# Flamingo block on one Trainium2 core: the weights of an expert block in one transfer instead of two, and two block tables built earlier

## The chip, the cores and the metric

The kernel runs on one core of one Trainium2 chip. The metric is the device time of one execution in microseconds (us). Each time named "span" is that of a profiled execution, from its first to its last instruction.

## The reference

The reference takes x of 8 x 256 x 128 floats (2048 tokens of 128 features) through four residual steps: a cross attention of 16 heads, a mixture-of-experts integrator of two iterations (8 experts, 2 per token), a second cross attention without weights, and a mixture of 8 gated experts. The change lies in the last step, and in how its work is laid out:

```python
def _L1_ffn_ref(x, Wr, br, W1, b1, W2, b2, W3, b3):
    E, D, DFF = (8, 128, 512)
    b, s, d = x.shape
    xt = x.reshape(b * s, d)
    logits = xt @ Wr + br
    pr, idx = jax.lax.top_k(logits, 2)
    w = jax.nn.softmax(pr, axis=-1)
    onehot = jax.nn.one_hot(idx, W1.shape[0], dtype=x.dtype)
    cw = jnp.einsum('tk,tke->te', w, onehot)
    y = jnp.zeros_like(xt)
    for e in range(W1.shape[0]):
        h = jax.nn.silu(xt @ W1[e] + b1[e]) * (xt @ W2[e] + b2[e])
        y = y + (h @ W3[e] + b3[e]) * cw[:, e:e + 1]
    return y.reshape(b, s, d)
```

## The kernel before

The 2048 tokens stand in four chunks of 512 (NC = 4, the last is called L). Each token has two experts, so there are 4096 rows. They are sorted by expert into `sorted_x` in DRAM, each expert's rows in a region of its own, and worked on in blocks of 128 rows of one expert, 39 in all (BLOCKS). The blocks don't wait for all tokens to be routed: a table gives the expert and the start row of each block, and it is made in three parts. The early table (9 blocks, EARLY) holds blocks that the first two chunks fill, the middle table (8) those that are full after the third chunk, the late table (22) the rest. Block numbers 9 and 17 are the first of the middle and of the late table.

What each engine does in the stretch of the blocks:

- TensorE, loop from L2265: for block j `up(j)` (eight products of 128 x 128 by 128, shown as 16 MATMULs in the trace, L2247), then `rows_T` (the transpose of a later block's rows, L2237), then `down(j - 1)` (L2258). The order is fixed in the code, so a wait of one of these holds all behind it. `up(j)` waits for the weights `w_in`, `rows_T(j)` for the rows `xb_in`. At a table border the transposes come later: `rows_T(9)` stands between `up(8)` and `down(7)`.
- ScalarE: the four silu of a block (L1087) and the copy of the transposed rows (L1078).
- VectorE, loop from L1649: the four `gated` products (L1655), then `keep_result(j - 1)` (L1647), and between them small pieces of routing: `choose(L)` at j = 2, `weights_of(L)` and `slots_of(L)` at j = 3 (the first waits for GpSimd's `w_top`, L804), `blocks_of(1)` at j = 4, the middle table at j = 5, `blocks_of(2)` at j = 7, the late table at j = 8.
- GpSimd, loop from L820: the indirect store of a block's result (L823), and between them the indirect stores of the third chunk's rows (L798, three before the loop, then two behind blocks 0 and 1 and one behind block 2), the power for the last chunk's weights `second_weights(L)` (L804) behind those of j = 1, and the last chunk's rows behind blocks 3 to 6.
- SyncE issues the loads, in the order of its program: for each block `load_weights` and `load_rows`. Each starts with a value load from the table (L598). The weights of a block are 772 KB, in two transfers: W1, W2 and the two biases (516 KB, L605) and W3 (256 KB, L608). There are four buffers (W_BUFS). From block 4 on, the first transfer waits for `gated` of four blocks ago, the second for the down product of four blocks ago. Rows (65 KB, L614) are loaded three blocks ahead (AHEAD). `load_blocks` (L633) starts a table: it waits for the table (the wait in L634), then issues weights, waits for the sent rows of that chunk, and goes on. The trace puts a block's value loads, and with them the wait for a table, at L598.

Of the kernel before, what the change touches and what calls it, by code (L numbers as in the profile page):

```python
# [50 lines left out]
B1_AT, B2_AT, W3_AT = 2 * FF, 2 * FF + MT, 2 * FF + 2 * MT  # L51
W_BUFS, X_BUFS = 4, 10
EARLY_CHUNKS = 2
EARLY = (2 * EARLY_CHUNKS * CH - E * (P - 1) + P - 1) // P
MIDDLE = (2 * (EARLY_CHUNKS + 1) * CH - E * (P - 1) + P - 1) // P - EARLY
# [24 lines left out]
def flamingo(nc, a, out):  # L80
    ctx = ExitStack()
    with ctx:
# [3 lines left out]
        def sem(name):  # L86
            return ctx.enter_context(nc.semaphore(name))
# [299 lines left out]
        shareT_ready = sem("shareT_ready")  # L387
        bias3_psum = sem("bias3_psum")
        w_in = [sem(f"w_in{i}") for i in range(W_BUFS)]
        w3_in = [sem(f"w3_in{i}") for i in range(W_BUFS)]  # L390
        xb_in = [sem(f"xb_in{i}") for i in range(X_BUFS)]
        xbT_psum = sem("xbT_psum")
        xbT_ready = sem("xbT_ready")
# [103 lines left out]
        def _(sp):  # L497
# [102 lines left out]
            def load_weights(j):  # L600
                expert = entry(j, 0, E - 1)
                w = a["wall"][bass.ds(expert, 1)].rearrange("o p n -> (o p) n")
                if j >= W_BUFS:
                    sp.wait_ge(gated_ready, MT * (j - W_BUFS + 1))
                sp.dma_start(wb[:, j % W_BUFS, 0:W3_AT], w[:, 0:W3_AT]).then_inc(w_in[j % W_BUFS], 16)  # L605
                if j >= W_BUFS:
                    sp.wait_ge(down_psum, j - W_BUFS + 1)
                sp.dma_start(wb[:, j % W_BUFS, W3_AT:], w[:, W3_AT:]).then_inc(w3_in[j % W_BUFS], 16)  # L608

            def load_rows(j):  # L610
                start = entry(j, 1, SLOTS - P)
# [53 lines left out]
        def _(pool):  # L665
# [135 lines left out]
            def second_weights(c):  # L801
                pool.wait_ge(gap2_ready, c + 1)
                tc = slice(c * TC, (c + 1) * TC)
                nc.gpsimd.tensor_tensor(w_top[:, tc, 1], euler[:, 0:TC], gap2[:, tc], ALU.pow).then_inc(w2nd_ready, 1)  # L804
# [15 lines left out]
            for j in range(BLOCKS):  # L820
                pool.wait_ge(yb_ready, j + 1)
                home = xb[:, j % X_BUFS, D:D + 1].bitcast(U32)
                nc.gpsimd.indirect_dma_start(sorted_y, bass.IndirectOffsetOnAxis(ap=home, axis=0), yb[:, j % X_BUFS, :],  # L823
                                             None).then_inc(yb_out[j % X_BUFS], 16)
                if j < 3:
                    send_rows(2, range(2 * j + 3, min(2 * j + 5, GR)))
                if j == 1:
                    second_weights(L)
                if 3 <= j < 7:
                    send_rows(L, range(2 * j - 6, 2 * j - 4))  # L830

# [270 lines left out]
        def _(dve):  # L1102
# [525 lines left out]
            choose(2)  # L1628
            weights_of(2)
            slots_of(2)  # L1630

            def expert_shares():

# [15 lines left out]
            for j in range(BLOCKS):  # L1649
# [14 lines left out]
                if j == 3:  # L1664
                    weights_of(L)
                    slots_of(L)
                if j == 4:
                    blocks_of(1)
                if j == 5:
                    table_of_blocks(1, middle_table, MIDDLE, middle_ready)  # L1670
                if j == 7:
                    blocks_of(2)
                if j == 8:
                    table_of_blocks(2, late_table, LATE, late_ready)
                if j == 10:
                    expert_shares()
# [15 lines left out]
        def _(pe):  # L1692
# [557 lines left out]

            def down(j):
                w = wb[:, j % W_BUFS, W3_AT:W3_AT + MT * D]
                pe.wait_ge(w3_in[j % W_BUFS], 16 * (j // W_BUFS + 1))
                pe.wait_ge(gated_ready, MT * (j + 1))
                if j:
                    pe.wait_ge(yb_ready, j)
                for m in range(MT):
                    last = nc.tensor.matmul(bank[4][:, 0:D], gated[:, j % 2, m, :], w[:, m * D:(m + 1) * D],  # L2258
                                            start=(m == 0), stop=(m == MT - 1))
                last.then_inc(down_psum, 1)  # L2260
# [133 lines left out]
```

## Time and profile before

| | us |
|---|---|
| median of 3 runs | 654.27 |
| lowest, highest | 643.7, 655.16 |
| the profiled execution, device time | 628.24 |
| its span | 626.4 |
| mean granted TensorE clock in it, share of full speed | 0.961 |

The views of the profile that are used: the page's digits, each the busy share of one fortieth of the span (15.7 us) in tenths; the waits, which name who stood idle and what ended the wait; the timelines of single engines, each line a start in us, a duration, the engine, the source line, the operation, the number of instructions merged, and in brackets the idle time before it with what ended it; and for a source line that issues transfers the time from issue to landing. A landing is not known for every transfer, so its median is that of those known.

### The profile page before, as it was taken

How to read it: one execution, taken by the hardware profiler on the slowest of the kernel's cores; microseconds unless marked ns; L12 is line 12 of the kernel's file. 1: busy time of each engine (PE TensorE's matmuls, PEld its weight loads, DVE VectorE, ACT ScalarE, POOL GpSimd, SP SyncE). 2: the span in 40 equal slices, each digit the busy share in tenths (PEclk: the TensorE clock that was granted, in tenths of full speed). 3: DMA queues.
4: the chain of work that ended last, by engine and by line, in shares of the span. 5: the costliest groups of instructions: out<-in, count | busy, mean ns of one | idle time of the engine just before them, and what ended most of it. 6: DMA issues, size and time to landing. Idle time of an engine off the chain costs nothing. (4 is left out here: it accounts for less than half of the span.)

```text
span 626.4 us, 10027 instructions
## 1 busy us (share of the span) xinstructions
PE 556.1 (89%) x3331; PEld 327.0 (52%) x3343; DVE 413.5 (66%) x1054; ACT 321.3 (51%) x652; POOL 206.9 (33%) x217
## 2 busy tenths in 40 slices
PE   3856899999998799999999999999977989999991
PEld 1422344444453244444444445545556978988981
DVE  4858978989348599677323665656887675444545
ACT  2624656666657875565445437274533534444430
POOL 4806801010023363001783220001465575323330
PEclk9886979999999999999999999999999899999996
DMA  8466693000019700000003002000003989989956
GB/s 277 119 172 103 160 197 53 2 4 3 2 65 321 258 0 1 1 0 0 0 16 119 0 1 20 0 1 0 23 25 112 288 263 296 311 278 321 321 208 209
DMA packets 48011, 71.21 MB, mean 114 GB/s; under 512 B 11110, under 2 KB 35112, under 8 KB 47672
## 3 DMA queue, kind: packets, MB, share of 16 engines
q1 hardware_dynamic: 44968, 65.61, 36.0%
q0 software_dynamic: 2272, 4.69, 2.1%
q8 instruction: 27, 0.44, 0.3%
q10 hardware_dynamic: 720, 0.27, 0.2%
q14 instruction: 24, 0.20, 0.1%
HBM read 59.18 MB, written 21.29 MB: 128 GB/s over the span
## 5 line engine op out<-in xcount | busy, mean ns | idle before, releaser
L1963 PE MATMUL psum<-hidden,ew 128*128 128x512 f32 x320 | 143.8, 592 | 0.6
L886 ACT ACTIVATE probs<-psum 128x512 f32<-128x512 f32 x128 | 74.6, 598 | 47.5 <-PE psum L1765 47.1
L1963 PEld LDWEIGHTS psum<-hidden,ew 128*128 128x128 f32 x320 | 60.7, 190 | 69.3 <-issue 68.1
L1172 DVE TENSOR_REDUCE negmax<-psum 128x4 f32<-128x1024 f32 x64 | 76.7, 1209 | 19.4 <-PE psum L1742 18.7
L2247 PE MATMUL psum<-xbT,wb 128*128 128x128 f32 x624 | 78.5, 280 | 3.0 <-DMA wb<-in_wall_dram 2.9
L2247 PEld LDWEIGHTS psum<-xbT,wb 128*128 128x128 f32 x624 | 74.3, 195 | 4.3 <-DMA wb<-in_wall_dram 4.1
L1087 ACT ACTIVATE silu_g<-psum,wb 128x128 f32<-128x128 f32 x156 | 44.6, 368 | 61.6 <-PE psum L2247 61.6
L1655 DVE SCALAR_TENSOR_TENSOR gated<-psum,wb,silu_g 128x128 f32<-128x128 f32 x156 | 43.9, 344 | 48.6 <-ACT silu_g L1087 46.5
L823 POOL DMA_INDIRECT sorted_y<-yb,xb x39 | 37.9, 972 | 66.8 <-DVE yb L1647 65.6
L1765 PE MATMUL psum<-stacks 50*128 50x256 bf16 x256 | 50.4, 287 | 4.1 <-issue 1.9
L768 POOL TENSOR_TENSOR hidden<-unmasked,chosen 128x512 f32<-128x512 f32 x16 | 24.5, 1534 | 60.1 <-ACT unmasked L936 59.0
L1778 PE MATMUL psum<-probs,v_aug 128*32 128x256 f32 x512 | 44.1, 409 | 0.0
L2258 PE MATMUL psum<-wb,gated 128*128 128x128 f32 x312 | 41.5, 276 | 1.5 <-DVE yb L1647 1.5
L2258 PEld LDWEIGHTS psum<-wb,gated 128*128 128x128 f32 x312 | 37.9, 192 | 2.0 <-issue 2.0
L798 POOL DMA_INDIRECT sorted_x<-xp,slot x32 | 31.8, 995 | 17.9 <-DVE slot L1529 9.6
L1349 DVE SCALAR_TENSOR_TENSOR soft<-psum,soft 128x512 f32<-128x512 f32 x24 | 16.2, 687 | 31.6 <-ACT soft L950 31.6
L1765 PEld LDWEIGHTS psum<-stacks 50*128 50x128 bf16 x256 | 18.8, 98 | 33.4 <-issue 16.8
L1742 PE MATMUL psum<-stacks 48*128 48x256 bf16 x256 | 30.7, 297 | 5.8 <-DMA stacks<-stacked 5.6
L1908 PE MATMUL psum<-xT,ew 128*128 128x512 f32 x64 | 32.8, 600 | 1.3 <-ACT routeT L908 1.3
L672 POOL TENSOR_SCALAR rstd<-meanvar 128x4 f32<-128x4 f32 x16 | 3.8, 240 | 89.5 <-DVE meanvar L1110 89.4
L962 ACT ACTIVATE sig_g<-psum 128x512 f32<-128x512 f32 x24 | 14.3, 596 | 35.1 <-PE psum L1963 35.1
L762 POOL TENSOR_TENSOR hidden<-hidden,chosen 128x512 f32<-128x512 f32 x16 | 22.2, 1416 | 20.1 <-DVE hidden L1336 20.1
(256 smaller groups left out, 955.5 us busy)
## 6 DMA issues: line engine op xcount, KB each, us to landing
wb<-in_wall_dram SPq DMA_DIRECT2D x39, 516.0 KB, 5.0
wb<-in_wall_dram SPq DMA_DIRECT2D x39, 256.0 KB, 4.4
sorted_x<-in_slots_dram SPq DMA_DIRECT2D x1, 9815.0 KB, 32.7
stacks<-stacked SPq DMA_DIRECT2D x12, 384.0 KB, 8.5
xb<-sorted_x SPq DMA_DIRECT2D x39, 65.0 KB, 3.7
stacked<-parts SPq DMA_DIRECT2D x6, 384.0 KB, 3.7
back<-sorted_y SPq DMA_DIRECT2D x4, 512.0 KB, 5.2
stacked<-parts SPq DMA_DIRECT2D x6, 256.0 KB, 3.6
```

The source lines that it names most:

```text
L798: nc.gpsimd.indirect_dma_start(sorted_x, bass.IndirectOffsetOnAxis(ap=slot[:, 2 * t + k:2 * t + k + 1], axis=0), xp[:, t, k, :], None).the ...
L823: nc.gpsimd.indirect_dma_start(sorted_y, bass.IndirectOffsetOnAxis(ap=home, axis=0), yb[:, j % X_BUFS, :], None).then_inc(yb_out[j % X_BUF ...
L886: nc.scalar.activation(probs[:, g % 2, h % 4, :, :], s2[n % 2].rearrange("p (k q) -> p k q", k=2), ACT.Exp, scale=float(HD) ** -0.5).then_ ...
L1087: nc.scalar.activation(silu_g[:, j % 2, m, :], bank[j % 2][:, m * P:(m + 1) * P], ACT.Silu, bias=wb[:, j % W_BUFS, B1_AT + m:B1_AT + m + 1 ...
L1172: nc.vector.tensor_reduce(negmax[:, p].rearrange("p h q -> p (h q)"), psum[:, i:i + 2, :].rearrange("p h (q k) -> p (h q) k", q=2), AX.X, ...
L1655: nc.vector.scalar_tensor_tensor(gated[:, j % 2, m, :], bank[2 + j % 2][:, m * P:(m + 1) * P], wb[:, j % W_BUFS, B2_AT + m:B2_AT + m + 1], ...
L1765: last = nc.tensor.matmul(s2[n % 2][:, k * S:(k + 1) * S], ks[rows, h // 2, b * S + k * P:b * S + (k + 1) * P], qs[rows, h // 2, b * S:(b ...
L1778: last = nc.tensor.matmul(o[b % 2][32 * j:32 * j + 32, (g // 2) * S:(g // 2 + 1) * S], v_aug[:, b % BC, k, 4 * g + j, :], probs[:, g % 2, ...
L1908: last = nc.tensor.matmul(dst, w[:, 0, :], xT[:, chunk(c)], start=True, stop=not it)
L1963: last = nc.tensor.matmul(dst, ew2[:, j, cols], hidden[:, c, k - 1, j, :], start=False, stop=(j == 3))
L2247: last = nc.tensor.matmul(bank[2 * i + j % 2][:, m * P:(m + 1) * P], w[:, i * FF + m * P:i * FF + (m + 1) * P], xbT[:, j % 2, :], start=Tr ...
L2258: last = nc.tensor.matmul(bank[4][:, 0:D], gated[:, j % 2, m, :], w[:, m * D:(m + 1) * D], start=(m == 0), stop=(m == MT - 1))
```

## The change

The two transfers of a block's weights become one, which waits for `gated` and for the down product of four blocks ago (for the latter last). The semaphores `w3_in` go; the down product waits for `w_in`, as the up product does. `blocks_of(1)` moves from block 4 to ahead of the loop, the middle table from j = 5 to j = 1, `blocks_of(2)` from j = 7 to j = 5, and the late table from j = 8 to j = 6. On GpSimd, `second_weights(L)` goes ahead of the two row sends of j = 1.

```diff
@@ load_weights (SyncE)
                 if j >= W_BUFS:
                     sp.wait_ge(gated_ready, MT * (j - W_BUFS + 1))
-                sp.dma_start(wb[:, j % W_BUFS, 0:W3_AT], w[:, 0:W3_AT]).then_inc(w_in[j % W_BUFS], 16)
                 if j >= W_BUFS:
                     sp.wait_ge(down_psum, j - W_BUFS + 1)
-                sp.dma_start(wb[:, j % W_BUFS, W3_AT:], w[:, W3_AT:]).then_inc(w3_in[j % W_BUFS], 16)
+                sp.dma_start(wb[:, j % W_BUFS, :], w[:, :]).then_inc(w_in[j % W_BUFS], 16)
@@ GpSimd's loop over blocks
+                if j == 1:
+                    second_weights(L)
                 if j < 3:
                     send_rows(2, range(2 * j + 3, min(2 * j + 5, GR)))
-                if j == 1:
-                    second_weights(L)
                 if 3 <= j < 7:
                     send_rows(L, range(2 * j - 6, 2 * j - 4))
@@ VectorE, ahead of its loop
             choose(2)
             weights_of(2)
             slots_of(2)
+            blocks_of(1)
@@ VectorE's loop
                 if j == 3:
                     weights_of(L)
                     slots_of(L)
-                if j == 4:
-                    blocks_of(1)
+                if j == 1:
+                    table_of_blocks(1, middle_table, MIDDLE, middle_ready)
                 if j == 5:
-                    table_of_blocks(1, middle_table, MIDDLE, middle_ready)
-                if j == 7:
                     blocks_of(2)
-                if j == 8:
+                if j == 6:
                     table_of_blocks(2, late_table, LATE, late_ready)
@@ down (TensorE)
-                pe.wait_ge(w3_in[j % W_BUFS], 16 * (j // W_BUFS + 1))
+                pe.wait_ge(w_in[j % W_BUFS], 16 * (j // W_BUFS + 1))
```

## Rows read from the trace of the kernel before

**Rows 1.** The page: the DMA engines' busy tenths by slice of 15.7 us.

```profile
DMA  8466693000019700000003002000003989989956
```

**Rows 2.** Waits from 485 to 612: total us, times, longest us.

```profile
PE psum L2237 <- DMA xb<-sorted_x: 4.8, 5, 2.0
...
PE psum L2247 <- DMA wb<-in_wall_dram: 2.9, 5, 1.2
```

**Rows 3.** Timeline of TensorE, at blocks 2, 5, 8, 10, 19, 20, 26, 27 and 38.

```profile
491.42 0.33 PE L2237 MATMUL psum<-ident,xb 128*128 128x128 f32 x1 [0.53 <-DMA xb<-sorted_x]
...
505.61 1.13 PE L2258 MATMUL psum<-wb,gated 128*128 128x128 f32 x8 [0.34 <-DVE yb L1647]
...
516.70 0.33 PE L2237 MATMUL psum<-ident,xb 128*128 128x128 f32 x1 [1.98 <-DMA xb<-sorted_x]
...
521.08 0.33 PE L2237 MATMUL psum<-ident,xb 128*128 128x128 f32 x1 [1.26 <-DMA xb<-sorted_x]
...
549.26 1.95 PE L2247 MATMUL psum<-xbT,wb 128*128 128x128 f32 x16
...
553.45 2.05 PE L2247 MATMUL psum<-xbT,wb 128*128 128x128 f32 x16 [1.24 <-DMA wb<-in_wall_dram]
...
572.41 1.95 PE L2247 MATMUL psum<-xbT,wb 128*128 128x128 f32 x16
...
574.30 1.06 PE L2258 MATMUL psum<-wb,gated 128*128 128x128 f32 x8
575.20 1.95 PE L2247 MATMUL psum<-xbT,wb 128*128 128x128 f32 x16
...
606.74 1.95 PE L2247 MATMUL psum<-xbT,wb 128*128 128x128 f32 x16
```

**Rows 4.** SyncE's own waits from 485 to 612: total us, times, longest us.

```profile
SPq L608 <- PE psum L2258: 8.0, 7, 1.7
SPq L598 <- DVE middle_table L1580: 2.5, 1, 2.5
```

**Rows 5.** Timeline of SyncE: issues for blocks 8, 9, 22 and 23.

```profile
506.91 0.33 SPq L608 DMA_DIRECT2D wb<-in_wall_dram  x1
...
512.14 1.44 SPq L614 DMA_DIRECT2D xb<-sorted_x  x2
...
555.22 0.34 SPq L605 DMA_DIRECT2D wb<-in_wall_dram  x1
555.74 0.33 SPq L608 DMA_DIRECT2D wb<-in_wall_dram  x1
...
557.94 0.34 SPq L605 DMA_DIRECT2D wb<-in_wall_dram  x1
```

**Rows 6.** Timeline of VectorE around blocks 0, 2, 4, 5 and 6.

```profile
489.03 1.12 DVE L1655 SCALAR_TENSOR_TENSOR gated<-psum,wb,silu_g 128x128 f32<-128x128 f32 x4 [2.08 <-PE psum L2247]
...
494.90 1.13 DVE L1655 SCALAR_TENSOR_TENSOR gated<-psum,wb,silu_g 128x128 f32<-128x128 f32 x4 [1.44 <-ACT silu_g L1087]
...
502.70 0.17 DVE L1510 TENSOR_SCALAR gap<-w_top 128x4 f32<-128x4 f32 x1 [1.23 <-POOL w_top L804]
...
508.04 0.16 DVE L1584 TENSOR_TENSOR ends<-ends,taken 128x8 f32<-128x8 f32 x1
...
510.27 1.13 DVE L1655 SCALAR_TENSOR_TENSOR gated<-psum,wb,silu_g 128x128 f32<-128x128 f32 x4
```

**Rows 7.** Timeline of GpSimd behind block 1's store.

```profile
500.64 0.96 POOL L798 DMA_INDIRECT sorted_x<-xp,slot  x1 [0.30 <-issue]
```

**Rows 8.** The chain that ended last: start, us, what (the rows of block 11).

```profile
516.07 4.96 DMA xb<-sorted_x
```

**Rows 9.** Line L608 (last 256 KB), issues from 568 to 612.

```profile
DMA to landing us min/median/max: 5.0/5.3/5.8
```

**Rows 10.** Line L605 (first 516 KB), issues from 568 to 612.

```profile
DMA to landing us min/median/max: 3.8/5.3/6.3
```

**Rows 11.** Line L608, issues from 512 to 550.

```profile
DMA to landing us min/median/max: 4.4/4.4/4.4
```

More of the change, by code:

```diff
@@ L389, in flamingo @@
         w_in = [sem(f"w_in{i}") for i in range(W_BUFS)]
-        w3_in = [sem(f"w3_in{i}") for i in range(W_BUFS)]
         xb_in = [sem(f"xb_in{i}") for i in range(X_BUFS)]
```

## The prediction

> **What bounds the kernel now.** I read the page first: its digits by slice show the DMA engines at 8 or 9 tenths from the 32nd slice to the 38th and nowhere else for so long [rows 1]. These are the 39 expert blocks, and everything the change touches lies there or just ahead of it. The waits of that stretch come next: TensorE stands still there 4.8 us for rows and 2.9 us for weights [rows 2]. The timeline of TensorE then says where, and how long a block takes when nothing is missing: from up(26) to up(27) 575.20 - 572.41 = 2.79 us [rows 3]. From up(19) at 549.26 to up(38) at 606.74 it takes 57.48 / 19 = 3.03 a block [rows 3]. So some 0.24 a block is lost late, and more in the first blocks and at the table borders. A block needs 772 KB of weights and 65 KB of rows; that the DMA digits stand at 9 [rows 1] says the transfers have little room either. Last, SyncE's own waits and timeline: it waits only 8.0 us for down products and 2.5 us for the middle table [rows 4], and between 555.22 and 557.94 it goes from one block's first weight transfer to the next in 2.72 us without a wait [rows 5]. It is a chain of value loads and three issues, nearly as long as a block, and when it is late (the weights of block 20, 1.24 us of wait at 553.45 [rows 3]) it can't catch up.
>
> **The change, part by part.**
>
> *One issue fewer.* The second issue starts 0.52 us behind the first (555.74 - 555.22 [rows 5]), so SyncE's chain falls from 2.72 to 2.20 us a block and is never the bound. In the first blocks it issues without waiting: the rows of block 3 come behind three weight loads, each with one issue less, 3 x 0.52 = 1.6 us earlier, and those of block 4 2.1 us earlier. TensorE waits 0.53 us for the first of them [rows 3] and nearly the same for the second; both go: -1.0.
>
> *Table work and GpSimd's order.* blocks_of(1) lands in front of block 0, where VectorE stands idle 2.08 us [rows 6]; it is five small operations, of which the trace's like take 0.16 to 0.3 us, at most 1.5 in all, so hidden. The middle table at j = 1 takes 2.2 us (508.04 to 510.27 [rows 6]) and falls into 1.44 us of idle time before 494.90 [rows 6]; gated(2) comes 0.8 us later, but down(2), which needs it, stands behind the whole of up(3), which has not begun: hidden. What now stands at j = 5 and 6, blocks_of(2) and the late table, takes the place of the middle table there, so nothing more is lost. second_weights(L) goes in front of two sends of 0.96 us each with 0.3 between [rows 7], 2.5 us earlier; VectorE's 1.23 us wait for it at 502.70 [rows 6] goes, and with it TensorE's 0.34 us at 505.61 [rows 3]. Two of GpSimd's row sends come 1.2 us later, the last one of the middle group does not, as it stood behind w_top already. With VectorE's other small shifts I count -0.5, so -1.5 by block 8.
>
> *The middle table's wait.* SyncE reaches the wait for the table behind the weights of block 8, at 506.91 + 0.33 = 507.3 [rows 5], and stands 2.5 us [rows 4]. That wait goes, but the weights of block 9 then wait for down(5). Down(4) ended at 505.61 + 1.13 = 506.74 [rows 3]; one block on, less the 1.5 us gained, down(5) ends at 508.0. So the weights go out at 508.2 and, half of SyncE's 2.2 us chain later, the rows of block 9 at 509.3 in place of 512.14 [rows 5]. From issue to transpose these took 516.70 - 512.14 = 4.6 us [rows 3, 5], which gives 513.8. TensorE wanted them at 516.70 - 1.98 = 514.7, now at some 512.9: 0.9 of the 1.98 us stay, and the transpose is 2.9 us earlier. The rows of block 11 sit behind the weights of block 10, which now wait for down(6), near 511.1: issued at 512.3, and 5.0 us later [rows 8] at 517.3, against 521.08 before [rows 3]. So block 10 starts 3.8 us earlier than before, of which 1.5 is counted: -2.3. At the border to the late table I count nothing: its rows stand behind a load that waited for a down product before too.
>
> *The later start of the weights.* Today the first 516 KB of block j may start at gated(j-4), and only the last 256 KB wait for down(j-4). Now all wait. SyncE issues 0.17 us behind a down product's end (505.61 + 1.13 = 506.74, and 506.91 [rows 3, 5]); that end lies 0.16 behind the next up's start (574.30 + 1.06 = 575.36 against 575.20 [rows 3]); up(j) comes two blocks behind this up. With p the time of a block and L the time from issue to landing, 2p = L + 0.37 with 0.04 from landing to start; and a block that wants 2.79 us allows L = 5.2. The merged transfer isn't in the trace. Bounds: no shorter than the second part alone, 5.3 in the last third [rows 9]; no longer than from the first issue to the second's landing, 0.5 + 5.3 = 5.8, with 6.3 as the longest of the first parts [rows 10]. Both parts land nearly together and the engines are busy, so bytes set it: I take 5.7, p = 3.03. Between 512 and 550 the second part landed after 4.4 [rows 11], so L = 4.9 and p stays 2.79: no wait there, nor in the early blocks.
>
> From up(19) to up(38) there are 19 periods. Block 20 keeps 1.0 of its 1.24 us (three row issues stand ahead of it in SyncE's chain). Four periods at 2.79 and fifteen at 3.03: 1.0 + 11.2 + 45.5 = 57.7 against 57.5: +0.2. SyncE's lateness is exchanged for a wait on the landing.
>
> The Trainium skill (DMA: Bandwidth & Descriptors, Anatomy of one DMA — SWDGE (gpsimd) path) gives a transfer about 2.0 us fixed plus its bytes at 436 GB/s, measured for the other issue path. That would be 3.8 us for these 772 KB. By it the 5.2 us are never reached and the fifteen periods cost 2.79. The trace does not agree: smaller parts took 5.3 here.
>
> **Sum.** -1.5 - 2.3 + 0.2 = -3.6 us. The profiled execution took 628.24 us (span 626.4 and 1.8 around it); it becomes 624.6. The runs' median is 654.27, 26 us over the profiled one, for which the trace gives no reason. I carry the difference over: 654.27 - 3.6 = 650.7.
>
> **Rivals.**
>
> *All hidden.* The merged transfer, with one start in place of two, lands in 5.2 us or less. Then 19 periods take 1.0 + 53.0 = 54.0, -3.5, and the whole -1.5 - 2.3 - 3.5 = -7.3: 647.0. For it: the 4.4 us of the middle stretch [rows 11]. Against: DMA engines at 9 tenths [rows 1]. Chance 0.2. The skill's fixed cost, above, would lead here.
>
> *Late weights (slower).* Every block now hangs on a landing that closes a loop of two blocks, and blocks are closer together before block 20 than they were, so queues are fuller. If L is 6.3, the longest seen [rows 10], p is 3.34 and the 19 periods take 63.5, +6.0; less 3.8 gained ahead, +2.2: 656.5. If blocks 12 to 19 go that way too, 8 x 0.55 = 4.4 more: 660.9. It decides from L = 6.1, where 19 periods cost what was gained. For it: landings rose from 4.4 to 5.3 as the blocks closed up [rows 9, 11]. Against: slower blocks load the engines less, which brings L down again. Chance 0.2.
>
> *The table is not the wait.* If the middle rows' sends, two of which come later, land behind SyncE's arrival, a wait for rows takes the place of the one for the table. The last send stands behind w_top and both of them in either order, so it is not later by its place; SyncE asks for it at 508.6, and another 1 us would be needed to bite. Then the -2.3 shrinks to nothing: -1.3, 653.0. Chance 0.1.
>
> **How the numbers follow.** My forecast, 650.7, has 0.5; its own range, L from 5.3 to 6.0, moves fifteen periods from 3.03 to 2.84 or 3.19, 647.8 to 653.1. The cases together reach from 647.0 to 660.9. The unprofiled runs of one program lie between 643.7 and 655.16, so the low end needs a few us below the cases: 642 to 660. Faster or slower by over 2% (13 us, about what a measurement of this kernel can tell from no change) lies outside every case: of the 127 us of this stretch 39 x 2.79 = 109 us are TensorE's at full pace, and the rest, 18 us, is all that there is to gain. I leave 0.05 for each, for what the trace doesn't show. The sign is more open than that: 0.75 for some gain.
>
> **What would show it.** Right, in the changed kernel: no wait of SyncE for the middle table; rows of block 9 issued some 3 us earlier; no 1.23 us wait of VectorE for w_top; SyncE waiting for down products in nearly every block, far over 8.0 us; TensorE's waits for rows down from 4.8 to about 1.5 to 2.5, its waits for weights at or above 2.9, spread over many small ones after block 24; landings of 772 KB near 5.7 us late and near 4.9 between. up(10) some 3.8 us earlier. Wrong: landings under 5.2 late (then all is hidden), or over 6.1 (then slower), a wait for the middle rows, or a new wait of TensorE on VectorE near blocks 2, 5 or 6 from the moved tables.

## The result, and the profile after

| | before | after |
|---|---|---|
| median, us | 642.2 (22 runs, 630.46 to 658.44) | 642.39 (22 runs, 635.56 to 661.68) |
| ratio after / before | | 1.0086, 95% interval 1.005 to 1.0123 |
| profiled execution, us | 628.24, span 626.4 | 636.66, span 634.9 |
| mean granted TensorE clock in it | 0.961 | 0.960 |

The change made the kernel 0.9% slower, some 5.5 us. That is within 2%, as forecast, but on the other side of zero: the forecast was -3.6 us. The ratio is of the executions alone in which the core was not in its slower state; the medians are of all 22, and so nearly alike.

The page after, the DMA engines' busy tenths by slice, which answers to [rows 1]:

```profile
DMA  8466792000059300000030001000117768899865
```

The waits of the kernel after from 485 to 620 (total us, times, longest us), which answer to [rows 2]; the up product is L2244 here, the transpose L2234, the down product L2255:

```profile
ACT silu_g L1085 <- PE psum L2244: 43.5, 26, 5.5
ACT silu_g L1085 <- issue: 22.4, 11, 3.0
DVE gated L1654 <- remote: 9.7, 2, 5.4
...
PE psum L2244 <- DMA wb<-in_wall_dram: 3.5, 8, 0.7
PE psum L2255 <- DVE yb L1646: 3.3, 3, 1.9
...
PE psum L2234 <- DMA xb<-sorted_x: 1.7, 2, 1.5
```

SyncE's own waits in the same stretch, which answer to [rows 4]:

```profile
SPq L605 <- PE psum L2255: 34.1, 25, 3.8
```

Much is as forecast. SyncE no longer waits for the middle table and waits 34.1 us for down products in place of 8.0; TensorE's waits for rows fell from 4.8 to 1.7 us and those for weights rose from 2.9 to 3.5, in small pieces. But two rows were not forecast: ScalarE waited up to 5.5 us for an up product and VectorE 5.4 us for a signal whose sender the trace does not name. Signals of this kind, that come several us after all that they need has ended, are called late signals below. From up(0) to up(10) this execution took 42.0 us and the one before 36.7; from up(10) to up(38) 87.9 and 84.6. So the first ten blocks, where the gain should be, seem to have lost 5 us, and the late ones 3.

One trace cannot say which of the two is the change. The experiments had to answer two questions: whose are the late signals in the first blocks, and what does the one transfer cost, which starts behind the down product.

### The profile page after: what moved, and what is told of

It reads as the page before. It is cut to its first block, busy times and chain, and to the rows that moved or that the text cites. A ratio compares the mean times of both kernels' runs of the same rounds, so it can differ in the third digit from the quotient of the medians.

```text
span 634.9 us, 9956 instructions
## 1 busy us (share of the span) xinstructions
PE 562.6 (89%) x3343; PEld 329.4 (52%) x3343; DVE 414.0 (65%) x1054; ACT 321.4 (51%) x652; POOL 206.9 (33%) x217
## 3 DMA queue, kind: packets, MB, share of 16 engines
q1 hardware_dynamic: 39352, 65.61, 35.3%
## 4 chain that ended last, share of the span: by engine, by line
PE 63%; DVE 10%; DMA 10%; SPq 7%; issue 4%; ACT 3%; POOL 2%; another core or an unknown queue 0%; DVEq 0%; POOLq 0%
PE psum L1960 21%; DMA wb<-in_wall_dram 5%; PE psum L2244 5%; PE psum L1905 5%; PE psum L1762 4%; PE psum L1775 4%; PE psum L2255 3%; PE psum L1907 3%; SPq L513 2%; PE psum L1957 2%; PE psum L1783 2%; PE psum L1739 2%; DVE negmax L1170 2%; DMA xb<-sorted_x 2%; PE psum L1789 1%
## 5 line engine op out<-in xcount | busy, mean ns | idle before, releaser
L1960 PEld LDWEIGHTS psum<-hidden,ew 128*128 128x128 f32 x320 | 60.7, 190 | 69.4 <-issue 68.1
L2244 PE MATMUL psum<-xbT,wb 128*128 128x128 f32 x624 | 81.2, 285 | 5.3 <-DMA wb<-in_wall_dram 3.5
L2244 PEld LDWEIGHTS psum<-xbT,wb 128*128 128x128 f32 x624 | 76.1, 199 | 8.0 <-DMA wb<-in_wall_dram 6.1
L2255 PE MATMUL psum<-wb,gated 128*128 128x128 f32 x312 | 41.8, 277 | 3.3 <-DVE yb L1646 3.3
L2255 PEld LDWEIGHTS psum<-wb,gated 128*128 128x128 f32 x312 | 37.9, 192 | 4.1 <-issue 3.9
L1905 PE MATMUL psum<-xT,ew 128*128 128x512 f32 x64 | 34.3, 626 | 0.0
L670 POOL TENSOR_SCALAR rstd<-meanvar 128x4 f32<-128x4 f32 x16 | 3.9, 241 | 89.4 <-DVE meanvar L1108 89.0
L960 ACT ACTIVATE sig_g<-psum 128x512 f32<-128x512 f32 x24 | 14.3, 596 | 35.1 <-PE psum L1960 35.1
```

Source lines behind the costliest of these rows:

```text
L1905: last = nc.tensor.matmul(dst, w[:, 0, :], xT[:, chunk(c)], start=True, stop=not it)
L1960: last = nc.tensor.matmul(dst, ew2[:, j, cols], hidden[:, c, k - 1, j, :], start=False, stop=(j == 3))
L2244: last = nc.tensor.matmul(bank[2 * i + j % 2][:, m * P:(m + 1) * P], w[:, i * FF + m * P:i * FF + (m + 1) * P], xbT[:, j % 2, :], start=Tr ...
```

## How the runs are compared

The span of an execution follows the granted clock: the kernel before took 633.2 us at a mean clock of 0.962 and 660.0 at 0.909 on one chip. Where the runs of a ratio happen to have unlike clocks, the plain ratio misleads: it is 1.022 for the kernel before against itself (e16, two runs). So each result below also has a "difference at equal clock": the kernels were measured in five groups, each on one chip and in one go, and for each group the spans of all runs were fitted with a parabola in the granted clock, common to its kernels, and one offset for each kernel against the kernel before. The offset is given in us with two standard errors.

A second column is read from the traces, the start of an up product to the start of another. The clock hardly touches these stretches: their rows show mostly the full pace of 1.95 us for the 16 products.

| kernel (edits) | ratio (95%) | difference at equal clock, us | up(0) to up(10) | up(10) to up(38) |
|---|---|---|---|---|
| **First chip** | | | | |
| e1 changed kernel | 1.0118 (1.0056 to 1.018) | +4.6 ± 1.7 | 45.4 | 87.5 |
| e2 merged transfer alone | 1.0201 (1.0163 to 1.0239) | +3.8 ± 1.9 | 41.9 | 88.8 |
| e3 tables and GpSimd's order alone | 1.0015 (0.9975 to 1.0054) | 0.0 ± 1.4 | 46.5 | 82.2 |
| e4 two transfers, both start late | 1.0051 (1.0003 to 1.0099) | +1.6 ± 1.5 | 42.6 | 89.4 |
| **Second chip** | | | | |
| e5 kernel before | | +1.6 ± 2.4 | 36.4 | 83.8 |
| e6 changed, five weight buffers | 0.9895 (0.9854 to 0.9935) | -6.7 ± 2.2 | 33.0 | 79.6 |
| e7 changed, rows ahead of weights | 1.0086 (1.0032 to 1.0141) | +3.7 ± 1.9 | 36.0 | 85.8 |
| e8 both edits of e6 and e7 | 0.9899 (0.9837 to 0.9961) | -4.2 ± 2.3 | 37.2 | 78.4 |
| **Third chip** | | | | |
| e9 kernel before | 1.0008 (0.9918 to 1.0098) | 0.0 ± 2.8 | 43.0 | 85.2 |
| e10 changed kernel | 1.0024 (0.9967 to 1.0081) | +3.6 ± 1.9 | 45.8 | 85.1 |
| e11 merged, five buffers, old tables | 0.9885 (0.9825 to 0.9944) | -4.8 ± 2.3 | 40.6 | 81.5 |
| e12 tables and order alone | 1.0014 (0.9942 to 1.0087) | +0.4 ± 2.2 | 44.9 | 82.0 |
| **Fourth chip** | | | | |
| e13 GpSimd's order alone | 0.9985 (0.9929 to 1.004) | -2.6 ± 1.5 | 35.3 | 84.9 |
| e14 tables alone | | +0.6 ± 2.3 | 34.5 | 84.2 |
| e15 changed kernel | 1.0048 (1.0001 to 1.0096) | +2.6 ± 1.6 | 34.0 | 88.7 |
| e16 kernel before | 1.022 (1.0164 to 1.0275) | -1.4 ± 3.1 | 36.2 | 83.4 |
| **Fifth chip** | | | | |
| e17 merged, five buffers, new order, old tables | 0.9895 (0.9703 to 1.0088) | -5.5 ± 2.3 | 35.1 | 79.0 |
| e18 changed, five buffers | 0.9815 (0.968 to 0.9951) | -8.7 ± 2.7 | 32.4 | 79.9 |

The changed kernel was measured three times beside the kernel before, on three chips: +4.6, +3.6, +2.6. Weighted by their errors that is +3.6 ± 1.0 us. Fitted with the runs at a clock of 0.94 and more alone they are +5.4 ± 1.7, +4.2 ± 1.9 and +3.1 ± 1.9, so the sign does not rest on the runs at a low clock. Only e2 has no run at 0.94 or more: its offset is the least certain of the table.

## Experiment: whose late signals are these?

The kernel before and the changed one, both unchanged, on the third chip and again on the fourth.

> The kernel before, unchanged, profiled beside the next three. Open is where the late signals in blocks 1 to 9 come from (in the profiles of the changed kernel, of the merged transfer alone, of the tables alone and of the split transfer started late, up(0) to up(10) took 42 to 46.5 us; in two profiles of the kernel before and three with other edits 33 to 37). If they belong to the chip or to the single execution, the kernel before can show them too: up(0) to up(10) over 41 us, where all kernels of this group show it. If they belong to the merged transfer or the moved tables, this one takes 36 to 37 us and the changed kernel beside it 42 or more. Compared at the same granted clock its span is within 2 us of the other runs of the kernel before.

> The changed kernel, unchanged, beside the kernel before on one chip. Theory (the late start of the weights, with the borders): at the same granted clock it is 3 to 6 us longer than the kernel before; up(19) to up(38) takes 57.2 to 58.2 us, up(10) to up(38) 86 to 88. If the late signals are the chip's, up(0) to up(10) is within 2 us of that of the kernel before beside it; if they are the change's, it is 4 us or more longer. Rival (the first blocks are what costs the time and the late ones nothing): up(10) to up(38) as in the kernel before.

The kernel before took 43.0 us from up(0) to up(10) here: it has the late signals too. These are its ScalarE and VectorE around block 7, timelines of two engines (the silu of block 7 is the first line):

```profile
517.03 1.14 ACT L1087 ACTIVATE silu_g<-psum,wb 128x128 f32<-128x128 f32 x4 [2.26 <-PE psum L2247]
522.84 1.14 ACT L1087 ACTIVATE silu_g<-psum,wb 128x128 f32<-128x128 f32 x4 [4.67 <-remote]
```

```profile
517.03 0.34 DVE L1647 TENSOR_SCALAR yb<-psum,xb 128x128 f32<-128x128 f32 x1
522.65 1.13 DVE L1655 SCALAR_TENSOR_TENSOR gated<-psum,wb,silu_g 128x128 f32<-128x128 f32 x4 [5.28 <-remote]
```

Silu(7) ends at 518.17, and gated(7), which needs nothing later, starts at 522.65, 4.5 us on. In the first profile of the kernel before, gated(7) came without a wait. The same kernel, again profiled on the fourth chip, does not have this:

> The kernel before again, for its profile on this chip. Whether up(0) to up(10) takes 36 to 37 us or 43 here tells which kind of chip this is; the three others are read against it. If the two kinds go by chip, all four kernels of this call show the late signals or none does.

> The changed kernel again, beside the parts. 3 to 5 us longer than the kernel before at the same granted clock; up(19) to up(38) 56.8 to 58.2 us. On a chip without the late signals up(0) to up(10) is 36 us or less, on one with them 42 to 46.

Here up(0) to up(10) took 36.2 us before and 34.0 after. All eight profiles on the first and the third chip show 40.6 to 46.5 us, all ten on the other three chips 32.4 to 37.2, whatever the kernel. The kernel before also has different times at equal clock there: at 0.95 the fits give it 636.5 and 635.9 us on the first and the third chip, 627.2, 628.7 and 628.4 on the others. So the late signals come with all kernels of a group or with none, not with an edit, and where they come the span is some 8 us longer, 6 to 7 of them in the kernel before from up(0) to up(10) (43.0 against 36.2 to 36.7). Each chip was measured in one go only, so whether it is the chip or the time is not separated; "chip" stands for both here. The profile after that is shown above has them and the one before has not. Read against each other without this control, the two would have put 5 us on the wrong account. What makes the signals late on such a chip the runs do not show.

On a chip with late signals the moved tables and order also seem to stretch the first blocks: 42.0, 45.4, 45.8 (changed kernel), 46.5 and 44.9 (tables alone) against 43.0, 41.9, 42.6 and 40.6 in four kernels with the old tables. It is one execution each and the groups overlap, so this stays a hint.

## Experiment: the parts of the change

The merged transfer alone (the change's edits to load_weights and down, and nothing else):

```diff
-                sp.dma_start(wb[:, j % W_BUFS, 0:W3_AT], w[:, 0:W3_AT]).then_inc(w_in[j % W_BUFS], 16)
                 if j >= W_BUFS:
                     sp.wait_ge(down_psum, j - W_BUFS + 1)
-                sp.dma_start(wb[:, j % W_BUFS, W3_AT:], w[:, W3_AT:]).then_inc(w3_in[j % W_BUFS], 16)
+                sp.dma_start(wb[:, j % W_BUFS, :], w[:, :]).then_inc(w_in[j % W_BUFS], 16)
```

> One transfer for the weights, tables and GpSimd's order as before. Late-weights theory: all of the loss is here; up(10) to up(38) takes 87 to 88 us as in the changed kernel, and the time is 1.005 to 1.012 of before. Moved-tables theory: the loss came with the tables; this one is at 0.995 to 1.002.

The moved table work and GpSimd's order alone, with two transfers as before:

```diff
+            blocks_of(1)
...
-                if j == 4:
-                    blocks_of(1)
+                if j == 1:
+                    table_of_blocks(1, middle_table, MIDDLE, middle_ready)
...
+                if j == 1:
+                    second_weights(L)
                 if j < 3:
                     send_rows(2, range(2 * j + 3, min(2 * j + 5, GR)))
```

> Tables and GpSimd's order as in the changed kernel, weights in two transfers as before. Late-weights theory: the tables by themselves gain what the prediction said, 1.5 to 3 us, so 0.995 to 0.998. Moved-tables theory: late signals in blocks 1 to 9 and 1.005 to 1.01.

And the whole again:

> The changed kernel itself, once more. Its first trace has signals that come late in blocks 1 to 9 (silu of block 5 starts 5.79 us behind its up product, where 1.09 is usual), and block 10 starts 5.1 us later than in the kernel before. One-off theory: the new trace has 1.09 to 1.2 there, and up(10) starts some 3 us earlier than in the kernel before. Theory that the change itself brings it: again lags of several us in blocks 4 to 8, up(10) some 5 us late. From up(10) to up(38) both expect 87 to 89 us against 84.6.

The merged transfer alone costs +3.8 ± 1.9, the tables and the order bring 0.0 ± 1.4, and the whole is +4.6 ± 1.7: within the errors the sum of its parts. The loss is in the merged transfer. The ratio of 1.0201 overstates it; all its runs but one (0.917) had a clock of 0.935 to 0.939, those of the kernel before up to 0.962.

The tables alone were taken apart further:

```diff
@@ GpSimd's loop (order alone)
+                if j == 1:
+                    second_weights(L)
                 if j < 3:
                     send_rows(2, range(2 * j + 3, min(2 * j + 5, GR)))
-                if j == 1:
-                    second_weights(L)
```

> The kernel before with GpSimd's order alone: second_weights(L) goes in front of two row sends of block 1, tables and transfers as before. My forecast gave it 0.5 us (VectorE's 1.23 us wait for w_top goes, TensorE's 0.34 us behind it). If it is right: -0.5 us at the same granted clock, within 1.5 us of zero, up(0) to up(10) as in the kernel before beside it, within 1 us. If this order is what makes the first ten blocks longer in the two traces of the moved tables (46.5 and 44.9 us against 43.0), up(0) to up(10) is 2 to 3 us longer here.

> The kernel before with the moved table work alone, GpSimd's order and two transfers as before. My forecast gave it 2.3 us, from the middle table's wait. If it is right: -2.3 us at the same granted clock, and no wait of SyncE for the middle table. If the table work between the first blocks is what lengthens them, up(0) to up(10) is 2 to 3 us longer than in the kernel before beside it and the time is within 1.5 us of it. In the two traces of tables and order together SyncE's wait was gone and the time was 0.0 and +0.4 us.

> The moved tables and GpSimd's order alone, two transfers as before. If they are worth what I predicted: -3 to -4 us at the same granted clock, and up(0) to up(10) 3 to 4 us shorter than in the kernel before beside it. If what they give early is waited off again later, up(0) to up(10) is 2 to 4 us shorter, up(10) to up(38) as much longer or the end hangs on something else, and the time is within 1.5 us. In the job before this one it came out at 0.0 us, with 1.4 us of uncertainty.

On the fourth chip up(0) to up(10) is 0.9 us shorter than in the kernel before beside it with the order alone, 1.6 with the tables alone, 2.2 with the whole change. With the tables alone SyncE no longer waits for the middle table (e14). So the step is there in the trace, in the forecast's direction, though in one execution each. The times say -2.6 ± 1.5 for the order (a plain ratio of 0.9985, 0.9929 to 1.004) and +0.6 ± 2.3 for the tables. Whether the order gave more than its 0.5 is not shown: fitted with the runs at a clock of 0.94 and more alone it is -2.1 ± 1.9. A gain of the tables is not to be seen in the time of a kernel with four buffers.

## Experiment: is it the start or the size?

Two transfers as before, but both behind the down product of four blocks ago. It leaves out the merge and keeps the late start:

```diff
                     sp.wait_ge(gated_ready, MT * (j - W_BUFS + 1))
-                sp.dma_start(wb[:, j % W_BUFS, 0:W3_AT], w[:, 0:W3_AT]).then_inc(w_in[j % W_BUFS], 16)
                 if j >= W_BUFS:
                     sp.wait_ge(down_psum, j - W_BUFS + 1)
+                sp.dma_start(wb[:, j % W_BUFS, 0:W3_AT], w[:, 0:W3_AT]).then_inc(w_in[j % W_BUFS], 16)
                 sp.dma_start(wb[:, j % W_BUFS, W3_AT:], w[:, W3_AT:]).then_inc(w3_in[j % W_BUFS], 16)
```

> Before, with the first transfer also waiting for the down product of four blocks ago, still two transfers. If the loss of the merged transfer is its later start, this one loses at least as much, as it keeps the second issue too: 1.008 to 1.015. If it is the merged transfer's size that makes it slow, this one is at 1.000 to 1.004, for the first part alone lands by 5.3 us.

From up(10) to up(38) it took 89.4 us, as long as the merged one on the same chip (88.8), while the kernel before took 83.4 to 85.2 in its four profiles, none of them in this group. In the time it is +1.6 ± 1.5, less than the merged one's +3.8 ± 1.9, with errors that overlap, and its ratio of 1.0051 lies between the two expectations. So the time does not decide between start and size. The traces show that the two kernels lose in different ways. Means over blocks 20 to 38, from the issues in SyncE's timeline and the products in TensorE's:

| | first weight transfer issued behind the end of down(j-4), us | from its issue to up(j), us |
|---|---|---|
| kernel before (first profile, e5, e9, e16) | 0.35 to 0.80 | 5.25 to 5.69 |
| merged transfer (first profile after, e1, e2, e10, e15) | 0.22 to 0.35 | 5.73 to 6.07 |
| e4, two transfers, both late | 0.97 | 5.13 |

In the late stretch the merged transfer is issued no later than the first part was in the kernel before, whose SyncE is late there: the issue that is saved makes up for the later wait. What is longer is the way from the issue to the up product, which now waits for all 772 KB and no longer for the first 516 alone. In e4 it is the other way round: SyncE has three issues a block and cannot run ahead, so it is late by itself (it waits for down products 9.1 us in 8 pieces; in e15 35.6 us in 30), and the way is the shortest. So e4's loss does not stand for that of the merged transfer. Between blocks 10 and 19 the merged transfer does start later: 0.42 us behind the down product in e15, where the first part went out 0.17 us ahead of it in e16.

## Experiment: a fifth buffer lets the transfer start a block earlier

With five buffers a load waits for the down product of five blocks ago, 2.8 us earlier, and nothing else is changed:

```diff
-W_BUFS, X_BUFS = 4, 10
+W_BUFS, X_BUFS = 5, 10
```

> The changed kernel with five weight buffers, so a transfer waits for the down product of five blocks ago, 2.8 us earlier. Late-weights theory: TensorE's waits for weights go, up(10) to up(38) falls from 87.5 to 79 to 82 us, and the time from 1.009 of before to 0.99 to 1.0. If the engines that move the data are the bound, the landings grow by what the start gained, and it stays at 86 to 88 us and 1.005 to 1.01.

It took -6.7 ± 2.2 us against the kernel before, with four buffers +3.6 ± 1.0. The waits of the execution from 485 to 620 (columns as above):

```profile
PEld psum L2234 <- DMA xb<-sorted_x: 6.1, 6, 2.0
...
PE psum L2234 <- DMA xb<-sorted_x: 3.4, 3, 1.8
```

TensorE's waits for weights are gone from the list, and every block from the 18th on takes 2.79 us (up(19) to up(38) 52.9). Yet the transfers still took about as long as four buffers allow or longer (5.2 us): 5.1 to 6.0 us, median 5.4, between 560 and 604, and 6.1 to 6.5 in its repetition below. They only start a block earlier: from issue to up product there are 7.87 us on average in blocks 20 to 38, against 6.07 in e15. So the loss is the wait for a landing that closes the loop, and it goes when the loop is made longer.

Five buffers with the old tables on the third chip:

> The kernel before with one transfer of weights per block and five buffers of weights in place of four; the table work and GpSimd's order as before. If the moved tables are worth what I predicted (2.3 us at the middle table and 1 to 1.5 ahead), this is 3 to 4 us longer than the changed kernel with five buffers, that is -3 us against the kernel before at the same granted clock, and SyncE waits 2 us or more for the middle table. If the tables are worth nothing, it is as fast as that one: -6 to -7 us.

It came to -4.8 ± 2.3, between the two expectations (-3, and -6 to -7), and tells them apart no better than that. SyncE waited 8.4 us for the middle table in its trace, so a wait of that size seems to be hidden to a large part when SyncE is ahead.

And on a fifth chip, without late signals, two kernels that differ in the tables alone:

> One transfer of weights per block, five buffers of weights, GpSimd's new order, and the table work where it was before the change. GpSimd's order alone gave -2.6 us (1.5 of uncertainty) and the five buffers with the merged transfer -4.8 to -6.7 at the same granted clock. If both add up: -7 to -9 us against the kernel before. If the moved tables are worth the 2.3 us that I forecast, this is 2 us longer than the next kernel, which has them too; if they are worth nothing, the two are within 2 us. up(19) to up(38) 52.9 us in both.

> The changed kernel with five buffers of weights, as in the second job, beside the kernel without its moved tables. -6.7 us against the kernel before in that job (2.2 of uncertainty); the same is expected here, and up(19) to up(38) 52.9 us with no wait of TensorE for weights after block 18. By the forecast's step for the middle table up(0) to up(10) is 2 us shorter here than in the kernel beside it.

SyncE's own waits in e17, from 505 to 625, and then in e18, from 485 to 620:

```profile
SPq L605 <- PE psum L2256: 18.6, 21, 2.0
SPq L651 <- DMA sorted_y<-yb,xb: 7.9, 1, 7.9
SPq L597 <- DVE middle_table L1578: 4.5, 1, 4.5
SPq L597 <- DMA sorted_x<-xp,slot: 1.4, 1, 1.4
```

```profile
SPq L605 <- PE psum L2255: 18.4, 18, 2.0
SPq L651 <- DMA sorted_y<-yb,xb: 15.0, 4, 7.9
SPq L659 <- DVE x L1686: 6.6, 4, 3.8
SPq L597 <- DMA sorted_x<-xp,slot: 2.7, 1, 2.7
```

With old tables SyncE stands 4.5 us before the middle table and 1.4 us for the sent rows. With the moved ones it does not wait for the table at all, and 2.7 us for the rows, which was the rival "the table is not the wait": 3.2 us less in sum. By the times e17 (-5.5) missed the -7 to -9 of both gains added, and e18 (-8.7) went beyond -6.7, both within their errors. The difference from up(0) to up(10) is 2.7 us (35.1 and 32.4), and in the time 3.2 us (-5.5 ± 2.3 and -8.7 ± 2.7). The time alone would not carry it; with the waits 3.2 us shorter and the stretch 2.7, in one execution each, the table's step of 2.3 us seems to have about the right size once the weights are not late. With 0.9815 (0.968 to 0.9951) e18 is the fastest version here; e6, the same kernel, has the narrower interval, 0.9895 (0.9854 to 0.9935).

A kernel with five buffers and two transfers was not run. The merge does away with one set of semaphores, but whether the fifth buffer needs that, and how much of the gain it would bring with two transfers, is open.

## Experiment: rows ahead of the weights at the borders

At a border the first rows stand behind the first weights in SyncE's order, and these now wait for a down product. The two rows were put ahead:

```diff
                 sp.wait_ge(table, 1)
-                load_weights(first)
                 sp.wait_ge(rows, 16 * GR)
                 load_rows(first)
                 load_rows(first + 1)
+                load_weights(first)
                 load_weights(first + 1)
```

> The changed kernel, with the first two row loads of a new table ahead of its first weights (four buffers). The row transfer of block 17 no longer waits for down(13): its transpose waited 1.5 us and up(16) to up(17) took 4.75 us. If rows queued behind the weights' wait are part of the loss, block 9 and 17 start 1 to 2 us earlier each, 2 to 3 us in all, ratio 1.003 to 1.007. If not, as the changed kernel, 1.009 to 1.012.

> Both: five buffers and the rows first. If the two terms add, 0.985 to 0.995 of before. If the transfers are the bound, 1.0 to 1.005.

+3.7 ± 1.9 and -4.2 ± 2.3 us, against +3.6 and -6.7 without the edit: no gain. The weights of block 9, now behind the rows, were the next thing late: up(9) waited for them 2.45 us in e7 and 3.94 us in e8. In these two executions the order of the queue at the border moved the wait and did not shorten it.

The kernel before again, on the second chip:

> The kernel before itself. The four new traces, of kernels with and without the merged transfer, all show signals that come late in blocks 1 to 9 and take 42 to 46.5 us from up(0) to up(10); the first trace of the kernel before took 36.7 without any. If the late signals belong to the execution or to the tracing and not to the edits, this trace has them too, 42 to 46 us. If they belong to the edits (each of the four has one of them), it is at 36 to 38 again. Ratio 0.995 to 1.005: it shows what the comparison itself scatters.

It took 36.4 us from up(0) to up(10), without late signals, like the three others on this chip. Beside the first chip alone that could have been read as the edits' doing; only the third chip, with the kernel before among the late ones, took them off the edits.

## Why the prediction was wrong, step by step

The clearest ledger is that of e16 and e15, before and after on one chip without late signals. TensorE's timeline of e16 (start, us, line, products) at up(0), the transpose of block 9, up(10), up(19), the wait of up(20), and up(38):

```profile
500.33 3.61 PE L2247 MATMUL psum<-xbT,wb 128*128 128x128 f32 x16
...
531.03 0.33 PE L2237 MATMUL psum<-ident,xb 128*128 128x128 f32 x1 [1.83 <-DMA xb<-sorted_x]
...
536.49 1.95 PE L2247 MATMUL psum<-xbT,wb 128*128 128x128 f32 x16
...
563.77 1.95 PE L2247 MATMUL psum<-xbT,wb 128*128 128x128 f32 x16
...
567.50 2.05 PE L2247 MATMUL psum<-xbT,wb 128*128 128x128 f32 x16 [0.78 <-DMA wb<-in_wall_dram]
...
619.84 1.95 PE L2247 MATMUL psum<-xbT,wb 128*128 128x128 f32 x16
```

and of e15 at up(0), the transpose of block 9, up(10), the wait of up(13), the transposes of blocks 17 and 19, up(19), up(28) and the wait of up(29), and up(38):

```profile
485.15 3.07 PE L2244 MATMUL psum<-xbT,wb 128*128 128x128 f32 x14
...
513.82 0.33 PE L2234 MATMUL psum<-ident,xb 128*128 128x128 f32 x1 [0.87 <-DMA xb<-sorted_x]
...
519.16 1.95 PE L2244 MATMUL psum<-xbT,wb 128*128 128x128 f32 x16
...
529.61 2.05 PE L2244 MATMUL psum<-xbT,wb 128*128 128x128 f32 x16 [0.98 <-DMA wb<-in_wall_dram]
...
541.13 0.33 PE L2234 MATMUL psum<-ident,xb 128*128 128x128 f32 x1 [1.21 <-DVE gated L1654]
...
544.86 0.33 PE L2234 MATMUL psum<-ident,xb 128*128 128x128 f32 x1 [0.60 <-DMA xb<-sorted_x]
...
548.95 1.95 PE L2244 MATMUL psum<-xbT,wb 128*128 128x128 f32 x16
...
576.30 2.05 PE L2244 MATMUL psum<-xbT,wb 128*128 128x128 f32 x16
...
580.08 2.05 PE L2244 MATMUL psum<-xbT,wb 128*128 128x128 f32 x16 [0.72 <-DMA wb<-in_wall_dram]
...
607.88 1.95 PE L2244 MATMUL psum<-xbT,wb 128*128 128x128 f32 x16
```

| stretch | e16 | e15 | difference | forecast |
|---|---|---|---|---|
| up(0) to up(10) | 36.2 | 34.0 | -2.2 | -3.8 |
| up(10) to up(19) | 27.3 | 29.8 | +2.5 | 0 |
| up(19) to up(38) | 56.1 | 58.9 | +2.9 | +0.2 |
| sum | 119.5 | 122.7 | +3.2 | -3.6 |

+3.2 in the trace, +2.6 ± 1.6 in the times on that chip.

This is one pair of executions. Over four profiles of each kernel (before: the first, e5, e9, e16; changed: the first, e1, e10, e15) up(10) to up(19) took 27.4 and 29.4 us on average, and up(19) to up(38) 56.8 and 58.0. So some 1.9 of the 3.1 us that these stretches lost lie between blocks 10 and 19, for which the forecast had nothing, and 1.1 behind.

**One issue fewer and GpSimd's order, -1.5: about right.** up(8) stands 26.9 us behind up(0) in e16 and 25.8 in e15, 1.2 less (1.6 against the first profile before). VectorE's wait for w_top and the one of 0.34 us behind it are gone. That there would be no wait for weights in the early blocks was wrong in a small way: up(8) waited 0.46 us for them, which the 1.2 already contain.

**The middle table's wait, -2.3: mechanism right, size too large.** The rows of block 9 were issued 2.5 us earlier (26.3 and 23.7 behind up(0); forecast 2.8), and their transpose came 2.0 us earlier, not 2.9, as they took 4.9 us from issue to transpose and not 4.6. The rows of block 11 took 5.6 where I had 5.0 by [rows 8]. So -1.0 between up(8) and up(10). Both are rows behind a transfer of 772 KB, and I had priced them with landings from a kernel with smaller ones; in e16 they took 4.4 and 4.8. (The working also has a slip: 514.7 less the 1.5 us gained is 513.2, not 512.9, which would leave 0.6 of the wait and not 0.9. It does not enter the sum; 0.87 stayed.)

**No wait between blocks 10 and 19: the step that failed first.** I took L = 4.9 there and concluded "p stays 2.79: no wait". The median landing was right: the transfers whose landing is known took 4.5 to 5.7 us, median 4.8, between 512 and 550. But a median under the limit of 5.2 does not keep every block under it. Block 13's weights were issued at 523.01 and its up product began at 529.61, after 6.6 us: 1.25 us against e16. The issue was not late. In e15 it came 0.22 us behind the end of down(9), in e16 that of the first part 0.18 us behind it (the down product, then the issue; e15 first):

```profile
521.72 1.07 PE L2255 MATMUL psum<-wb,gated 128*128 128x128 f32 x8
523.01 0.34 SPq L606 DMA_DIRECT2D wb<-in_wall_dram  x1
```

```profile
539.33 1.06 PE L2258 MATMUL psum<-wb,gated 128*128 128x128 f32 x8
540.57 0.34 SPq L605 DMA_DIRECT2D wb<-in_wall_dram  x1
```

But in e16 the first part landed after 3.8 us, and up(13) came 5.2 us behind the issue without a wait. Nor is a lost microsecond given back, since the next issue hangs on the later down product.

**"At the border to the late table I count nothing": wrong by 1.3 us.** Blocks 17, 18 and 19 took 4.33, 3.62 and 3.02 us in e15 against 4.01, 2.91 and 2.79. The rows of block 19 were issued in time, at 540.11, but needed 4.75 us to the transpose in e15 and at most 3.27 in e16, where it did not wait for them: they are queued behind the merged transfer of block 18. (The profile puts the 1.21 us of block 17's transpose down to a gated product, but in the code it waits only for its rows and for the copy before it; the rows went out at 536.77, 4.4 us before.) In the first profile after, block 17 took 4.75 us against 3.71 in the first profile before, with these lines of TensorE's timeline:

```profile
545.96 2.05 PE L2244 MATMUL psum<-xbT,wb 128*128 128x128 f32 x16 [0.35 <-DMA wb<-in_wall_dram]
549.53 0.33 PE L2234 MATMUL psum<-ident,xb 128*128 128x128 f32 x1 [1.52 <-DMA xb<-sorted_x]
```

**The loop after block 19, +0.2: mechanism right, L mis-sized.** SyncE's timeline of e15 shows the issues of the weights of blocks 28 and 29:

```profile
570.20 0.34 SPq L606 DMA_DIRECT2D wb<-in_wall_dram  x1
571.29 0.34 SPq L612 DMA_DIRECT2D xb<-sorted_x  x1
573.75 0.34 SPq L606 DMA_DIRECT2D wb<-in_wall_dram  x1
```

Down(25) ended at 573.53, the weights of block 29 went out 0.22 us later, and up(29) started at 580.08, that is 6.3 us behind the issue and 0.72 late. In e16 the first part for block 29 went out as close behind down(25), at 588.58, and landed after 4.1. The known landings from 568 to 606, in the forecast's terms:

```profile
DMA to landing us min/median/max: 5.6/6.1/6.6
```

Forecast 5.7. 5.7 came from the first and the second part of before (5.3, 5.3 and up to 6.3 [rows 9, 10]). The merged transfer's median of 6.1 lies near their longest, not near their middle; in e16 both parts again had 5.3 and 5.2. The loop 2p = L + 0.37 with 6.1 gives 3.24 us a block where the loop binds; over up(20) to up(38) e15 took 3.12, as the loop does not bind in every block: six of these up products waited for weights, 3.4 us in all. With 6.1 the forecast's own working for 19 periods gives 1.0 + 11.2 + 15 x 3.24 = 60.7; measured were 58.9, 58.2, 58.0 and 56.8 in four executions of the changed kernel, against a forecast of 57.7. The absolute number was nearly met. What was missing was that the kernel before does better than its first profile: 57.5 there, 57.2, 56.6 and 56.1 in three others. "SyncE's lateness is exchanged for a wait on the landing" took the size of one execution's lateness as lasting. And "Block 20 keeps 1.0 of its 1.24 us" was wrong: from up(19) to up(20) the four profiles of the kernel before took 3.6 to 4.2 us, those of the changed one 2.8 to 3.0. This wait went, which brought some 1 us that the forecast did not count, and hid a part of what the longer landings cost.

The Trainium skill (DMA: Bandwidth & Descriptors, Anatomy of one DMA — SWDGE (gpsimd) path) would have given 3.8 us for this transfer, as an estimate from its figures. The trace does not agree: 4.5 to 5.7 us in the earlier stretch and 5.6 to 6.6 in the later one, beside rows and stores, with the DMA engines at 8 to 9 tenths.

**The rivals.** "Late weights (slower)" came, with its decision point L = 6.1 met nearly exactly: it had 0.2. (It took the long period for all 19 blocks, where the forecast took it for 15; by the forecast's working L = 6.1 costs 3.2 us and not 4.0.) What counted against it, "slower blocks load the engines less, which brings L down again", was too weak if it was there at all. "The table is not the wait" is seen in e18 (2.7 us for the sent rows) without eating the gain. The range of 642 to 660 held the median of 642.39 only because the runs of both kernels were 12 us faster than those the forecast was counted from (642.2 against 654.27); by difference, +3.6 ± 1.0 was inside the cases for the slower side (+2.2 to +6.6).

## What to carry to other kernels

Before a transfer is made to wait for a later event, or is merged with another so that the first consumer waits for all of it, work out the loop that it closes (here issue, landing, up, down, issue: two blocks) and compare the longest landings of that stretch with what the loop allows, not the median: what goes over the limit was not won back here. An issue less on a queue is worth its 0.5 us only where that queue is late. A buffer more (here -8 to -12 us at the same other edits) was worth more than any order of issues that was tried. And profile the kernel before again beside the one after before explaining a difference between two traces.

## What the runs showed of the hardware

- The same program took some 8 us of 630 more on two of five chips at the same mean granted clock (636 against 627 to 629 us at 0.95). There signals between engines came up to 5 us late in a stretch of some 20 us, the one in which GpSimd issues its indirect stores in close succession, mostly 0.3 us apart. Whether those have to do with it, and what else is slower there, is open.
- The span falls with the mean granted clock by some 3.3 to 4.6 us for each 0.01 near 0.95, far more than most edits here are worth: a comparison of runs with unlike clocks says nothing about such an edit.
- Rows of 65 KB queued right behind a transfer of 772 KB on the same queue took 4.9 and 5.6 us from issue to use at blocks 9 and 11 and 4.4 and 4.75 at blocks 17 and 19 (e15). Behind two smaller transfers the same rows took 4.4 and 4.8, 4.1 and at most 3.3 (e16).
- A weight transfer of 772 KB landed 4.5 to 5.7 us after its issue (median 4.8) from 512 to 550 in e15 and 5.6 to 6.6 (6.1) from 568 to 606, where the DMA engines were busy 8 to 9 tenths. In e16 the first 516 KB landed after 3.7 to 5.9 (4.1) from 530 to 563 and 4.1 to 6.0 (5.3) from 580 to 618.
